# Attention scores with triangular masks on quarters of the array, added after the scores

## The reference

```
def _alibi_causal_mask(S, dtype):
    q = jnp.arange(S)[:, None]
    k = jnp.arange(S)[None, :]
    return jnp.where(k <= q, -(q - k).astype(dtype), NEG_INF)
...
scores = jnp.einsum('bhqd,bhkd->bhqk', q, k) / np.sqrt(hd)
scores = scores + _alibi_causal_mask(S, scores.dtype)
probs = jax.nn.softmax(scores, axis=-1)
```

## Time and profile before

| | |
|---|---|
| device time, median of 3 runs | 1598.38 us (1597.86 to 1601.06) |
| profiled execution: device time | 1599.05 us |
| profiled execution: span of the core | 1597.0 us |
| PE busy | 1476.2 us (92%) |
| DVE busy | 1264.5 us (79%) |
| ACT busy | 1147.3 us (72%) |
| GpSimd busy | 868.1 us (54%) |
| DMA queue of the transfers | 49.4% of 16 engines |
| granted TensorE clock, mean | 0.975 |

### The profile page before, as it was taken

How to read it: one execution, slowest core, us unless ns; L and a number is a source line. 1 busy time by engine, 2 the same in 40 slices (tenths; PEclk the granted TensorE clock), 3 DMA queues, 4 the chain that set the end, 5 groups by cost and what they waited for, 6 DMA issues and landing times.

```text
span 1597.0 us, 56175 instructions
## 1 busy us (share of the span) xinstructions
PE 1476.2 (92%) x21460; PEld 946.3 (59%) x21460; DVE 1264.5 (79%) x3013; ACT 1147.3 (72%) x2466; POOL 868.1 (54%) x935
## 2 busy tenths in 40 slices
PE   5788999999999999999999999999999999999874
PEld 4355666666666666665666666655666666566542
DVE  4577888888888888888888888887888888888722
ACT  0177777877787777777777877777787777777751
POOL 1113556655565566556655665564566556555555
PEclk8799999999999999999999999999999999999987
DMA  3335545456556554555555545545455554555521
GB/s 113 96 114 158 162 149 168 144 159 178 165 160 176 149 164 144 163 175 153 175 170 155 163 145 164 171 146 173 152 162 141 168 171 155 175 159 146 148 79 30
DMA packets 196945, 241.06 MB, mean 151 GB/s; under 512 B 22238, under 2 KB 147110, under 8 KB 196678
## 3 DMA queue, kind: packets, MB, share of 16 engines
q1 hardware_dynamic: 196684, 237.48, 49.4%
HBM read 135.06 MB, written 101.81 MB: 148 GB/s over the span
## 4 chain that ended last, share of the span: by engine, by line
PE 64%; DMA 10%; DVE 9%; issue 6%; SPq 5%; ACT 4%; POOL 2%; POOLq 0%; DVEq 0%; ACTq 0%
PE ps L512 26%; PE ps L611 12%; PE ps L606 8%; PE ps L663 6%; PE ps L658 5%; DMA qk_d<-qk_st 5%; DMA kz<-qk_d 3%; DVE mxp L885 3%; PE ps L626 2%; PE ps L528 2%; ACT prob L692 2%; SPq L363 1%; DVE ve_c L810 1%; DVE st_c L796 1%; DVE zr L897 1%
## 5 line engine op out<-in xcount | busy, mean ns | idle before, releaser
L885 DVE TENSOR_REDUCE mxp<-ps 128x4 f32<-128x512 f32 (+1 forms) x1536 | 842.8, 593 | 164.8 <-PE ps L626 160.0
L692 ACT ACTIVATE prob<-ps 128x512 f32<-128x512 f32 (+1 forms) x1536 | 732.0, 525 | 120.6 <-PE ps L611 114.9
L611 PE MATMUL ps<-qs,kz 50*128 50x128 f16 (+2 forms) x3584 | 404.0, 239 | 13.1 <-DVE mxp L885 11.0
L626 PE MATMUL ps<-kz,qs 49*128 49x128 f16 (+1 forms) x4096 | 409.5, 231 | 0.1
L611 PEld LDWEIGHTS ps<-qs,kz 50*128 50x128 f16 x3584 | 260.8, 94 | 87.3 <-ACT prob L692 31.3
L626 PEld LDWEIGHTS ps<-kz,qs 49*128 49x128 f16 x4096 | 286.2, 95 | 4.0 <-DVE mxp L885 1.6
L1022 POOL TENSOR_TENSOR om<-oc,rz 128x512 f32<-128x512 f32 x64 | 79.9, 1269 | 333.0 <-DMA rz<-rz_d 333.0
L663 PE MATMUL ps<-prob,va 128*32 128x384 f32 (+2 forms) x3072 | 237.2, 381 | 0.0
L606 PE MATMUL ps<-mk 64*128 64x256 bf16 x1024 | 198.0, 273 | 36.9 <-ACT prob L692 15.1
L658 PE MATMUL ps<-prob,va 128*32 128x128 f32 x4096 | 209.3, 276 | 0.6 <-ACT prob L692 0.3
L622 PE MATMUL ps<-mk 64*128 64x256 bf16 x1024 | 200.5, 276 | 7.8 <-DMA kz<-qk_d 5.1
(11 more groups left out here) (124 smaller groups left out, 2855.2 us busy)
## 6 DMA issues: line engine op xcount, KB each, us to landing
qk_d<-qk_st SPq DMA_DIRECT2D x128, 256.0 KB, 2.8
ou_d<-ou SPq DMA_DIRECT2D x128, 256.0 KB, 2.3
qs<-qk_d SPq DMA_DIRECT2D x256, 96.0 KB, 2.4
kz<-qk_d SPq DMA_DIRECT2D x256, 96.0 KB, 2.5
xa<-in_L_attn_x SPq DMA_DIRECT2D x32, 512.0 KB, 5.3
qk_d<-qk_st SPq DMA_DIRECT2D x128, 128.0 KB, 3.4
xc<-in_L_attn_x SPq DMA_DIRECT2D x32, 512.0 KB, 4.4
oc<-ou_d SPq DMA_DIRECT2D x32, 512.0 KB, 4.9
```

The costliest lines, as they stand in the source:

```text
L611: x_ = mm(bank[:, col:col + w * P], kz[rows, h // 2, kt * P:(kt + 1) * P], qs[rows, h // 2, qt * P:(qt + w) * P], start=(n > 0), stop=(n > ...
L626: x_ = mm(bank[:, col * P:(col + w) * P], qs[rows, h // 2, qt * P:(qt + 1) * P], kz[rows, h // 2, kt * P:(kt + w) * P], start=(n > 0), sto ...
L692: nc.scalar.activation(prob[:, h % 8, at:at + w], ps[:, ST + n, 0:w], ACT.Exp, scale=1.0 / FS).then_inc(s["exp_done"], 1)
L885: v.tensor_reduce(mxp[:, g % 2, at, first:first + apart * (BLOCKS[n] - 1) + 1:apart], bank.rearrange("p (m k) -> p m k", k=P), AX.X, ALU.m ...
```

## The change

Three things change in the scores of bank 0.

1. The order: the four squares on the diagonal come first (the first with `start=True`), the two mask matmuls last, added to them.
2. The shape: a mask matmul has 64x64 weights (the triangle alone) and writes a quarter of each square, partitions and columns 0 to 63 (m = 4) or 64 to 127 (m = 5). It still has 256 columns to stream, 64 for each of the four squares. The framework gives it an array tile of 64 rows by 64 columns.
3. The quarters: of the two quarters off the diagonal of a square one is wholly allowed and needs no mask; the other is wholly masked and gets its mask through four spare rows of the contraction. In row r (one for each of the four token tiles) `kz` holds -65504 for the tokens in the second half of tile r, `qs` holds 65504 for those in the first half, and zero elsewhere, so that a late key with an early query of the same tile adds -4.3e9 to the score. The contraction grows from 50 to 54 rows in `score` and from 49 to 53 in `row_score`.

```
-MX_ROWS = 49
-ST_ROWS = 50
+BAR_ROWS = 4
+MX_ROWS = PARTS + 1 + BAR_ROWS
+ST_ROWS = MX_ROWS + 1
...
+BAR = 65504.0
...
-        mk = sb("mk", [P, 4 * P + 4 * HALF], BF16)
+        mk = sb("mk", [P, 6 * HALF], BF16)
...
-            return mk[:, u * P:(u + 1) * P]
+            return mk[:, u * HALF:(u + 1) * HALF]
...
-                sp.dma_start(kz[at:at + 2, :, :], kaug_d).then_inc(s["kaug_loaded"], 16)
-                sp.dma_start(qs[at:at + 1, :, :], qaug_d).then_inc(s["kaug_loaded"], 16)
+                sp.dma_start(kz[at:at + 2 + BAR_ROWS, :, :], kaug_d).then_inc(s["kaug_loaded"], 16)
+                sp.dma_start(qs[at:at + 1 + BAR_ROWS, :, :], qaug_d).then_inc(s["kaug_loaded"], 16)
...
-                if n == 0 and m < 2:
-                    x_ = mm(bank.rearrange("p (t k) -> p t k", t=QT)[:, :, HALF * m:HALF * m + HALF], mask_key(2 + m)[half],
-                            EYE[half].rearrange("p (t k) -> p t k", t=QT), start=(m == 0), stop=False)
+                if n == 0 and m >= QT:
+                    at = slice(HALF * (m - QT), HALF * (m - QT) + HALF)
+                    x_ = mm(bank.rearrange("p (t k) -> p t k", t=QT)[at, :, at], mask_key(1)[half],
+                            EYE[half].rearrange("p (t k) -> p t k", t=QT), start=False, stop=True)
...
                     x_ = mm(bank[:, col:col + w * P], kz[rows, h // 2, kt * P:(kt + 1) * P],
-                            qs[rows, h // 2, qt * P:(qt + w) * P], start=(n > 0), stop=(n > 0 or m == 5))
+                            qs[rows, h // 2, qt * P:(qt + w) * P], start=(n > 0 or m == 0), stop=(n > 0))
...
-    kaug = np.full((2, 8, 512), FS, np.float16)
-    kaug[0] = np.arange(512) * (FS / QONE)
-    qaug = np.full((1, 8, 512), QONE, np.float16)
+    tok = np.arange(512)
+    tile = (tok[None, :] // P == np.arange(BAR_ROWS)[:, None])[:, None, :]
+    late = (tok % P >= HALF)[None, None, :]
+    kaug = np.full((2 + BAR_ROWS, 8, 512), FS, np.float16)
+    kaug[0] = tok * (FS / QONE)
+    kaug[1:1 + BAR_ROWS] = np.where(tile & late, -BAR, 0.0)
+    qaug = np.full((1 + BAR_ROWS, 8, 512), QONE, np.float16)
+    qaug[1:1 + BAR_ROWS] = np.where(tile & ~late, BAR, 0.0)
```

More of the change, by code:

```diff
@@ L232, in build @@
         wo_f = vst[:, 2:4, :]
-        m_nat = om[:].rearrange("p a b -> p (a b)")[:, 0:4 * P + 4 * HALF]
+        m_nat = om[:].rearrange("p a b -> p (a b)")[:, 0:6 * HALF]
         ow_t = vst[:, 0:2, :]
@@ L320, in mask_key @@
         def mask_key(u):
-            return mk[:, u * P:(u + 1) * P]
-        EYE = mk[:, 4 * P:4 * P + 4 * HALF]
+            return mk[:, u * HALF:(u + 1) * HALF]
+        EYE = mk[:, 2 * HALF:6 * HALF]
         @block.sync
@@ L604, in score @@
                 bank = ps[:, ST + n, :]
-                if n == 0 and m < 2:
-                    x_ = mm(bank.rearrange("p (t k) -> p t k", t=QT)[:, :, HALF * m:HALF * m + HALF], mask_key(2 + m)[half],
-                            EYE[half].rearrange("p (t k) -> p t k", t=QT), start=(m == 0), stop=False)
-                else:
-                    kt, qt, w = CHUNK[n][m - 2 if n == 0 else m]
-                    col = sum(c[2] for c in CHUNK[n][:m - 2 if n == 0 else m]) * P
+                if n == 0 and m >= QT:
+                    at = slice(HALF * (m - QT), HALF * (m - QT) + HALF)
+                    x_ = mm(bank.rearrange("p (t k) -> p t k", t=QT)[at, :, at], mask_key(1)[half],
+                            EYE[half].rearrange("p (t k) -> p t k", t=QT), start=False, stop=True)
+                else:
+                    kt, qt, w = CHUNK[n][m]
+                    col = sum(c[2] for c in CHUNK[n][:m]) * P
                     x_ = mm(bank[:, col:col + w * P], kz[rows, h // 2, kt * P:(kt + 1) * P],
-                            qs[rows, h // 2, qt * P:(qt + w) * P], start=(n > 0), stop=(n > 0 or m == 5))
+                            qs[rows, h // 2, qt * P:(qt + w) * P], start=(n > 0 or m == 0), stop=(n > 0))
                 if m == (MOVES[n] if n < 2 else 1) - 1:
@@ L620, in row_score @@
                 bank = ps[:, MX + n, :]
-                if n == 0 and m < 2:
-                    x_ = mm(bank.rearrange("p (t k) -> p t k", t=QT)[:, :, HALF * m:HALF * m + HALF], mask_key(m)[half],
-                            EYE[half].rearrange("p (t k) -> p t k", t=QT), start=(m == 0), stop=False)
+                if n == 0 and m >= QT:
+                    at = slice(HALF * (m - QT), HALF * (m - QT) + HALF)
+                    x_ = mm(bank.rearrange("p (t k) -> p t k", t=QT)[at, :, at], mask_key(0)[half],
+                            EYE[half].rearrange("p (t k) -> p t k", t=QT), start=False, stop=True)
                 else:
-                    qt, kt, w, col = ROWS_AT[n][m - 2 if n == 0 else m]
+                    qt, kt, w, col = ROWS_AT[n][m]
                     x_ = mm(bank[:, col * P:(col + w) * P], qs[rows, h // 2, qt * P:(qt + 1) * P],
-                            kz[rows, h // 2, kt * P:(kt + w) * P], start=(n > 0), stop=(n > 0 or m == 5))
+                            kz[rows, h // 2, kt * P:(kt + w) * P], start=(n > 0 or m == 0), stop=(n > 0))
                 if m == MOVES[n] - 1:
@@ L1081, in constants @@
     row = at % HALF
[L1082 to L1085, removed]
-    kaug = np.full((2, 8, 512), FS, np.float16)
-    kaug[0] = np.arange(512) * (FS / QONE)
-    qaug = np.full((1, 8, 512), QONE, np.float16)
+    part = np.arange(HALF)
+    keys = np.where(part[None, :] < row[:, None], NEG, 0.0)
+    queries = np.where(part[None, :] > row[:, None], NEG, 0.0)
+    eye = np.tile(np.where(row[:, None] == part[None, :], 1.0, 0.0), (1, 4))
+    mask = np.concatenate([keys, queries, eye], axis=1).astype(np.float32)
+    tok = np.arange(512)
[6 more added lines that the diff above has]
+    qaug[1:1 + BAR_ROWS] = np.where(tile & ~late, BAR, 0.0)
     return {"ident": np.eye(P, dtype=np.float32), "mask": mask, "kaug": kaug, "qaug": qaug}
```

## The result

The changed kernel takes 1631.49 us (median of 4 runs, 1629.64 to 1633.46) where the kernel before takes 1598.12 (median of 4, 1595.98 to 1601.06). The ratio is 1.020, with a 95% interval of 1.0178 to 1.0222: 33 us slower. The forecast was 1635 us and slower.

The account below looks back on a forecast made before the run. PE was taken as the bound; 0.08 us more in each of 520 groups gave 42 us, taken as 37, less 0.3 for setup, from 1599.05 to 1635.8, 0.67 lower for the median: 1635 us, range 1588 to 1656 (0.83).

Parts of the forecast that it names:

- What bounds: Whole kernel: PE is the bound, busy 523.9 of 540 us between 460 and 1000 us, nothing else near it.
- Overlap: Masks in bank 0: four quarter matmuls run as one group of 256 columns, 0.12 us instead of 0.23, gaining 0.11.
- Edges: Changes of tile form around the bank 0 masks: 0.09 us lost on the way in, 0.10 on the way out.
- the rows of L506 and of L564: Trace evidence for column-only form changes: L506 in setup loses 0.09 us each way, transpose L564 nothing; the forecast followed L506.
- The sum: Each slot's masks: 0.09 + 0.12 + 0.10 = 0.31 us against 0.23, 0.08 more; 42 us for 520 groups.
- The share on the path: At least 0.84 of PE's added time lengthens the run: 35 us as floor, 42 as ceiling, 37 taken.
- The forecast's own hint: PE's waits once or twice in a batch, 0.54 us in the one shown or 0.36 for DVE, can give back a little.
- bank 0 ready at the old place: Bank 0's end in a slot: 0.43 us behind the slot's start against 0.45 before, so ACT and DVE begin as before.
- the constants for nothing: Setup: the constants' DMAs are a few rows more, issued long before the wait for the mask conversion ends, costing nothing.
- Column halves do not overlap: Rival, bank 0 masks: two matmuls of one row half run in sequence, 0.19 us more a slot, 1681 to 1698; chance 0.05.
- One switch is hidden: Rival, edges of the masks: form change costs only one way, slot gains 0.01 to 0.02 us, 1590 to 1594; chance 0.07.
- No switch cost: Rival, edges of the masks: column-only changes cost nothing, slot gains 0.11 us, 1545 to 1565, say 1553; chance 0.12.

Follow-up runs that it names:

- the third pair of masks: Kernel before the change plus a third pair of full-width masks in bank 0 of every slot, with no added change of form; 1.018 of the kernel before.
- the kernel with one change of form: Changed kernel with the four squares of bank 0 also split into column halves, banks 1 and 2 left in 64x128 tiles; 1.002 of the kernel before.
- The pairs of masks added by place: Kernel before plus the extra full-width mask pair only in slots 0, 1, 3, 10 to 15 (1.0153), or only in 2, 4 to 9 (1.0056).
- the kernel with all scores in quarters: Changed kernel with every matmul of scores split into two column halves, so all tiles in the slot are 64x64; 0.9934 of the kernel before, 0.9919 when repeated.

## Why the prediction was right, and where it was off

**What bounds.** PE is the bound for what is added: shown by the third pair of masks, which adds PE time alone and makes 1.018.

**Overlap.** The 0.11 us gained is there: four masks within 0.01 us. The comparison that the forecast rested on was weaker than it had to be. It set weighted sums in f32 (0.027 us each) against an fp16 matmul (0.055). For f32 on the whole array the rows of L503 have 0.215 us for 256 columns, so 0.11 for 128. Against that the four column tiles overlapped four to one.

**Edges.** The choice between the rows of L506 and of L564 was the right one. A change of columns alone costs, 0.09 us in. Out it was 0.12, where I took 0.10 and gave 0.11 as the upper end. In the kernel with one change of form the same step costs 0.10 (0.20 to 0.21 less 0.107). There the masks follow squares of their own form, here they are the first group behind a change, and the first group behind a change is slower in the traces shown: by 0.01 us for a pair (0.065 us for the first pair of squares here; 0.12 and 0.11 for the two mask pairs in the earlier trace rows), by 0.02 for a group of four (0.08 from the first squares in quarters to the second, 801.72 to 801.80 and 804.80 to 804.88). I had the pair in the starts of the earlier trace rows and rounded it away.

**The sum.** The slot was forecast with 0.08 us and measured with 0.12: about 0.02 more on the way out, 0.01 in the block of 384 columns behind it, the rest rounding. I applied it to all slots. In slots 4 and 5 side steps (`t2`, `v`) stand between bank 0 and bank 1, and the change of form behind the masks was there already. (From the first matmul of bank 0 to bank 1, slot 4 takes 1.14 us before and 1.15 after. Slot 5 can't confirm it: its period, 4, also stands still with the third pair, so a wait covers it.) So 14 of 16 slots pay: 520 x 14/16 x 0.12 = 55 us on PE instead of the forecast 42.

**The share on the path.** This is the step that failed. I called 0.84 of PE's added time a floor, "since the chain can only be replaced by a longer one". Measured are 33 of 55 us, 0.61, and 0.52 for the third pair. The count behind the 0.84 was right: piece by piece, the chain passes through the masks in 155 of 189 slots (0.82), and in the changed kernel still in 126 of 183. But the chain of one execution is no such floor. One reason is that it gives to PE slots in which PE waits. Slot 2 shows it, first in the kernel before, then in the changed one:

```profile
763.86 0.27 PE L606 MATMUL ps<-mk 64*128 64x256 bf16 x1
...
764.24 0.21 PE L611 MATMUL ps<-qs,kz 50*128 50x128 f16 x1
...
764.45 0.32 PE L611 MATMUL ps<-qs,kz 50*128 50x384 f16 x1
```

```profile
777.82 0.23 PE L614 MATMUL ps<-qs,kz 54*128 54x128 f16 x1
...
778.15 0.29 PE L609 MATMUL ps<-mk 64*64 64x256 bf16 x1
...
778.38 0.33 PE L614 MATMUL ps<-qs,kz 54*128 54x384 f16 x1
```

Before, bank 1 comes 0.21 us behind the last square instead of 0.055. In all 26 batches it starts there 0.15 us behind the end of a `maxima`, so PE waits for DVE. The view marks no wait, because the square's busy time, 0.21 us to its modelled end, covers it, and the chain goes through PE. With the change the slot takes 0.56 us up to bank 1 like the others, 0.03 less than the 0.60 it had: the added time went into the wait, and period 1 even got shorter.

The rest went into waits that the view does mark; why the chain did not run through them already before is not shown. The forecast's own hint, was such a place: the one in the earlier trace rows has become

```profile
828.81 0.27 PE L614 MATMUL ps<-qs,kz 54*128 54x256 f16 x1 [0.18 <-DVE mxp L889]
```

and over the whole execution PE's idle time before the blocks of bank 2, first before, then after (form, count, busy and mean, idle and its releasers):

```profile
L611 PE MATMUL ps<-qs,kz 50*128 50x256 f16 x512 | 138.8, 271 | 12.0 <-DVE mxp L885 11.0 <-ACT prob L692 0.6
```

```profile
L614 PE MATMUL ps<-qs,kz 54*128 54x256 f16 x512 | 139.4, 272 | 5.8 <-DVE mxp L889 5.0 <-ACT prob L696 0.8
```

Before bank 0, where the kernel before has its masks and the changed one its squares, again first before, then after:

```profile
L606 PE MATMUL ps<-mk 64*128 64x256 bf16 x1024 | 198.0, 273 | 36.9 <-ACT prob L692 15.1 <-DMA kz<-qk_d 15.0 <-DVE mxp L885 5.2
L622 PE MATMUL ps<-mk 64*128 64x256 bf16 x1024 | 200.5, 276 | 7.8 <-DMA kz<-qk_d 5.1 <-DVE mxp L885 2.5
```

```profile
L630 PE MATMUL ps<-kz,qs 53*128 53x128 f16 x3584 | 385.4, 220 | 7.1 <-DMA kz<-qk_d 5.6 <-DVE mxp L889 1.3
L614 PE MATMUL ps<-qs,kz 54*128 54x128 f16 x2560 | 313.0, 218 | 27.5 <-DMA qs<-negm 9.2 <-ACT prob L696 7.9 <-DMA kz<-qk_d 5.7
```

The waits for the new keys fell from 20.1 to 11.3 us, but those for the row of maxima, at the same place, rose from 1.5 (in the view of waits) to 9.2, so the two together hardly changed. What fell is the wait for ACT before bank 0, 15.1 to 7.9, and the one before bank 2, 12.0 to 5.8. In all, PE's time without busy work went from 120.8 to 103.9 us of the span, 17 of the 22 us that do not show. Slot 2 makes up about the other 5 (0.15 us in each of 32 batches, from the 0.11 not paid and the 0.04 that period 1 lost). The pairs of masks added by place (0.79 and 0.37) agree that the time is given back in certain places.

So 37 us was forecast from a slot term a third too small and a share a third too large, and the two errors met at 33. That the time fell into the range owes something to this.

**Small terms.** Masks of other values for nothing: the exponential of 512 columns has 595 ns and the maximum 682 ns in both kernels. Nothing in the traces speaks against bank 0 ready at the old place and the constants for nothing. The spare rows cost nothing that can be measured. The conversion of `mk` went from 0.56 to 0.36 us, 0.2 of the forecast 0.3.

**The signs.** Of the signs given, four masks within 0.02 us, 0.15 us to the first mask and a shorter wait for `kz` came; from the last mask to bank 1 it was 0.23 instead of 0.21. One failed: the masks' share of the chain was to grow and fell from 9.2% to 5.2%. The run with the full-width masks behind the squares had 5.8%, so most of this comes from the masks no longer opening the slot.

**The rivals.** "Column halves do not overlap" is out by the timeline of the changed kernel. "One switch is hidden" is out too, both are paid. "No switch cost" is out for the change; its premise, that 64x128 and 64x64 share their row split and so cost nothing, is refuted in the same rows. The traces agree with the Trainium skill's rule that a change of tiling mode drains the engine (TensorEngine Tiling (Array Packing), Tiling Modes, Key Properties), all but the transpose L564: here the change costs 0.09 us in and 0.10 to 0.12 out.

## What to carry to other kernels

Small tiles pay if the work around them has the same form: here four quarter matmuls save 0.11 us, and the two changes of form around them cost 0.21. Count the changes of form along the program, those that are there already included, before counting the columns saved. Look for waits in the distance between starts too: in slot 2 of the kernel before, one of 0.15 us stood in no idle time, since a modelled end covered it. And do not take the share of a line in one execution's chain as the share of a change that will show: add a known amount of the same engine's time, place by place, and measure, in the direction of the change; here additions showed with 0.37 to 0.79 of their size by place, and removals with a quarter to a third.

## What the runs showed of the hardware that was not expected

In the kernel with all scores in quarters, PE starts 16 matmuls with 16 weight loads in about 0.22 us for the four squares, 14 ns each, and within a group of four the starts lie some 3 ns apart. The Trainium skill (TensorE: Matmul & The Clock Gate, the section "Wait — 56ns, not 53.3ns?") gives some 25 ns from start to start as a lower limit for matmuls however small. The trace of the changed kernel agrees for 128x128 tiles, with 25 ns between matmuls of 8 columns (L514, 838.00 to 838.12). For matmuls on different tiles the 3 and 14 ns differ from it, and the measurement decides.

The small transpose L564, with weights of 16 columns, costs no change of form between 128x128 matmuls: it starts 0.11 us behind one, and in the changed kernel (there L566, 846.06) the next starts 0.11 behind it. L506 with 32 columns has such a cost. Whether this is because it is a transpose or because of its 16 columns was not tried.
